# Attention in a Perceiver block: softmax weights stationary, values streaming

## The chip, the cores and the metric

The kernel runs on one core of a Trainium2 chip. The metric is device microseconds of one execution; three runs of the kernel before took 2517.41, 2518.72 and 2515.10, median 2517.41. Each TensorE product here is a stationary operand (loaded into the array by its own instruction, LDWEIGHTS) and a moving operand that streams past, column by column, into PSUM.

## The reference, cut to what matters

The block is a cross attention from 512 latent tokens to 8192 context tokens, then a state-space (Mamba) layer, a gated MLP and a mixture of experts. Only the attention changes:

```python
# Q: normalised latents (1, 512, 512); K = V = context (1, 8192, 512); 16 heads of 64
q = (scale * (Q @ Wq + bq)).reshape(bs, q_len, NH, DM)
k = (K @ Wk + bk).reshape(bs, kv_len, NH, DM)
v = (V @ Wv + bv).reshape(bs, kv_len, NH, DM)
a = jax.nn.softmax(jnp.einsum('nlhd,nshd->nhls', q, k), axis=-1)
o = jnp.einsum('nhls,nshd->nlhd', a, v).reshape(bs, q_len, NH * DM)
return o @ Wo + bo
```

Everything is kept near float32 accuracy on a float16 array: each operand is split into a high half and a low half (the rest), both float16, and a product is high x high, high x low and low x high (`three`, `product`).

## The kernel before, in words

Scratch memory in DRAM passes results between stages. `latent_queries` makes the queries, `context_keys_values` makes keys and values of all 8192 context tokens in 16 chunks of 512 (`kd` and `vd`, high and low halves, and a row maximum per query for the softmax), `attention` follows, then the Mamba stage, the MLP and the experts. Each engine runs its own program, written by hand in order; semaphores hold it where it needs another's result.

In `attention` a head has 32 steps (`HP`), each of two key tiles of 128 keys against all 512 queries. For a step:

- TensorE makes the scores of both tiles (`scores`, L938 and L939), keys stationary, queries moving: four matmuls of 512 columns into one of three PSUM buffers `st`.
- ScalarE takes the exponential of the two tiles in one operation of 1024 columns into `pf` (float32, a ring of 4 steps, `FULL`), L771.
- The high half `ph` (a ring of 8, `RING`) is a copy to float16: ScalarE in even steps (L765), VectorE in odd ones (L814, `DVE_HI`). The low half `pl` is `pf - ph`, always VectorE, L818.
- TensorE adds weights times values (`values`): values stationary, weights moving. The stationary block of a key tile is 128 columns, 64 of the value's high half and 64 of its low half: two 512-column matmuls with `ph` (L900); four with `pl` and 32 columns of the high half each, in four column strips of the array (L907); and four with a block of ones, which give the softmax's sums (L915).

TensorE works by groups of four steps (`SP`): the scores of a group, then the values of the group before (`LAG` = 1 group). A loop over the heads runs from one cut in a head to the same cut in the next (`turns`, `pair_turns`), so a head's end lies inside the next head's steps.

At a head's end VectorE copies the accumulator to SBUF (L824, L825). SP's queue sends the sums to DRAM and the two halves of the output to `a0` and `a1`; once per pair of heads the sums come back spread over partitions, VectorE adds them and takes the reciprocal, SP spreads it over 64 partitions each, and VectorE and ScalarE scale the output and split it into `oh` and `ol` (`reciprocals`, `scale`, `high`, `low`). After the last head `oh` and `ol` are projected with 96 matmuls on TensorE, and normalisation follows.

SP's queue loads the next head's keys and values in quarters, as the present head is done with them (L635, L640). In the first head the same queue also holds the other heads' queries, the biases and a zero fill of `xs_dram` for the experts (L653 to L659).

Of the kernel before, what the change touches and what calls it, by code (L numbers as in the profile page):

```python
# [90 lines left out]
WT = TW * (NCK // 2 - 1)  # L91

# [166 lines left out]
def context_keys_values(nc, keep, ctxT, q_dram, kd, vd, m_dram, mrow, m_out, wpack, wsplit):  # L259
# [6 lines left out]
    with ExitStack() as ctx:  # L266
# [4 lines left out]
        vs = [m.sb(f"vs{i}", [P, NH, CK // P, 2 * DH], F16) for i in range(2)]  # L271
# [11 lines left out]
        made = m.sem("made")  # L283
# [33 lines left out]
        def _(sp):  # L317
# [12 lines left out]
            def chunk(g, par, i, tiles, more):  # L330
# [6 lines left out]
                at = g * CK if isinstance(g, int) else i * (2 * CK) + (2 - par) * CK  # L337

                for js in (range(0, 6), range(6, 8)) if isinstance(g, int) and g == NCK - 1 else (range(0, 8),):
# [4 lines left out]
                    sp.dma_start(vd.rearrange("h p s -> p h s")[:, :, bass.ds(at + kts.start * P, len(js) // 2 * P)],  # L344
# [9 lines left out]
            for e in range(TW):  # L354
                load_weights(0, e)
            chunk(0, 0, None, (), True)
# [14 lines left out]
        def _(pool):  # L371
            def chunk(g, par, uses, i, tiles):
                nxt = 1 - par
                for n in range(8):
# [11 lines left out]
                    nc.gpsimd.tensor_tensor(vs[par][:, hs, kt, DH:2 * DH],  # L386
# [8 lines left out]

            identity(nc, pool, ident, made)
# [154 lines left out]
FULL = 4  # L551

SUMS_AT, SCALE_AT, HIGH_AT, LOW_AT, CUT = 8, 14, 16, 18, 20
EPS1, EPS2 = 1e-5, 1e-6
LAG = 1

HP = KT // 2
SP = 4
HS = HP // SP

# [3 lines left out]
DVE_HI = (1, 3, 5, 7)  # L564


def act_highs(n):

    return n // 8 * (8 - len(DVE_HI)) + sum(k not in DVE_HI for k in range(n % 8))


def attention(nc, keep, x, q_dram, m_dram, mrow, m_out, kd, vd, sums, r_dram, bv, bo, n1w, wsplit, xs_dram):
# [3 lines left out]
    with ExitStack() as ctx:  # L576
# [4 lines left out]
        vs = m.sb("vs", [P, KT, P], F16)  # L581
        ones = m.sb("ones", [P, 32], F16)
        pf = m.sb("pf", [P, FULL, 2, T])
        ph, pl = (m.sb(n, [P, RING, 2, T], F16) for n in ("ph", "pl"))
        parts = m.sb("parts", [P, 2, T])
# [4 lines left out]
        both = [m.sb(n, [P, 2, TT]) for n in ("both_var", "both_sd", "both_rs", "both_tmp")]  # L590
        oh, ol = (keep.big[0][:, i * 2 * WC:(i + 1) * 2 * WC].rearrange("p (j t) -> p j t", t=T) for i in range(2))
        a0, a1, rb, bob = (keep.big[1][:, i * 2 * T:(i + 1) * 2 * T].bitcast(F32) for i in range(4))
        dn = keep.big[1][:, 8 * T:8 * T + 64].bitcast(F32).rearrange("p (n c) -> p n c", c=8)
# [13 lines left out]
        pl_ready, pv_done, acc_read, o_out = (m.sem(n) for n in ("pl_ready", "pv_done", "acc_read", "o_out"))  # L607
        dn_in, r_ready, r_out, rb_in = m.sem("dn_in"), m.sem("r_ready"), m.sem("r_out"), m.sem("rb_in")
        own_dve, consts, vec_in, small_in = m.sem("own_dve"), m.sem("consts"), m.sem("vec_in"), m.sem("small_in")
        s_ready, oh_ready, ol_ready, y_ready = m.sem("s_ready"), m.sem("oh_ready"), m.sem("ol_ready"), m.sem("y_ready")  # L610
# [11 lines left out]
        FK = SP * 2 * P  # L622
# [8 lines left out]
        def _(sp):  # L631
# [7 lines left out]
            def load_values(n, q):  # L639
                sp.dma_start(vs[:, q * 2 * QP:(q + 1) * 2 * QP, :].rearrange("p k c -> p (k c)"),  # L640
                             vd.rearrange("h p s -> p h s")[:, bass.ds(n, 1), q * QK:(q + 1) * QK]
                             .rearrange("p h s -> p (h s)")).then_inc(v_in[q], 16)
# [19 lines left out]
            def load_next(h):  # L662
# [6 lines left out]
            def store(j, e):  # L669

                h = 2 * j + e
                sp.wait_ge(acc_read, 2 * h + 4)
                sp.dma_start(sums[:, bass.ds(h * T, T)],
                             parts[0:P:32, 1, :]).then_inc(o_out, 16)
                for n, a in enumerate((a0, a1)):
                    sp.dma_start(a[e * DH:(e + 1) * DH, :], parts[n * DH:(n + 1) * DH, 0, :]).then_inc(o_out, 16)

            def factors(j):


                sp.wait_ge(o_out, j * 96 + 144)
                sp.dma_start(dn, sums.rearrange("n (j p c) -> j p n c", p=P, c=8)[bass.ds(j, 1)]
                             .rearrange("o p n c -> p (o n) c")).then_inc(dn_in, 16)
                sp.wait_ge(r_ready, j + 1)
                sp.dma_start(r_dram.rearrange("(j p c) -> j p c", p=P, c=8)[bass.ds(j, 1)]
                             .rearrange("o p c -> p (o c)"), dn[:, 0, :]).then_inc(r_out, 16)
                sp.wait_ge(r_out, j * 16 + 16)
                for e in range(2):
                    sp.dma_start(rb[e * DH:(e + 1) * DH, :],
                                 r_dram[bass.ds(j * (2 * T) + e * T, T)].partition_broadcast(DH)).then_inc(rb_in, 16)  # L690

            with sp.Fori(0, PAIRS - 1) as j:
                for e in range(2):
                    load_next(2 * j + e)
                    store(j, e)
                factors(j)
            load_next(NH - 2)
            store(PAIRS - 1, 0)
            sp.wait_ge(st_ready, (NH - 1) * HP + 2 * QP)
            load_split(sp, wsplit, W.O, k_cur[:, 0:2 * WC], k_one[:, 0:2 * WC], w_in)  # L700
            sp.wait_ge(pl_ready, NH * HP + RING)
            sp.dma_start(xs, x.rearrange("(t p) d -> p t d", p=P)).then_inc(small_in, 16)
            store(PAIRS - 1, 1)
            factors(PAIRS - 1)
# [6 lines left out]
        def _(pool):  # L711
            own = Chain(pool, const_ready)
            own.done(nc.gpsimd.memset(ones[:, :], 1.0))
# [7 lines left out]
        def turns(eng, step, steps, cut, end=None):  # L721


            for s in range(cut):
                step(0, s)
            with eng.Fori(0, NH - 1) as h:
                for s in range(cut, steps + cut):
                    step(h, s)
                if end:
                    end(h)  # L730
            for s in range(cut, steps):
                step(NH - 1, s)
            if end:
                end(NH - 1)

        def pair_turns(eng, step, end, late, once):

            for s in range(CUT):  # L740
                step(0, s)
            once()
            with eng.Fori(0, PAIRS - 1) as j:
                for e in range(2):
                    for s in range(CUT, HP + CUT):
                        step(2 * j + e, s)
                        if s == HP + 2:
                            end(2 * j + e)
                        if e and s - HP in late:
                            late[s - HP](j)  # L750
            for s in range(CUT, HP + CUT):
                step(NH - 2, s)
                if s == HP + 2:
                    end(NH - 2)
            for s in range(CUT, HP):
                step(NH - 1, s)
            end(NH - 1)

        @block.scalar
        def _(act):  # L760
            def hi(h, s):
                g = h * HP + s
                act.wait_ge(pf_ready, g + 1)
                act.wait_ge(pv_done, g + 1)
                nc.scalar.activation(ph[:, s % RING, :, :], pf[:, s % FULL, :, :], ACT.Copy).then_inc(ph_ready, 1)  # L765
# [10 lines left out]
            def high(j):  # L776
                act.wait_ge(s_ready, j + 1)
                nc.scalar.activation(oh[:, bass.ds(j, 1), :].rearrange("p o t -> p (o t)"), a0, ACT.Identity,
                                     bias=bvs[:, bass.ds(j, 1)]).then_inc(oh_ready, 1)
# [5 lines left out]
            pair_turns(act, pair, lambda h: None, {HIGH_AT: high}, lambda: act.wait_ge(consts, 2))  # L785
            high(PAIRS - 1)
# [7 lines left out]
        def _(dve):  # L794
# [14 lines left out]
            def pair(h, s):  # L809
                g = h * HP + s  # L810
                if s % 8 in DVE_HI:
                    dve.wait_ge(pf_ready, g + 1)
                    dve.wait_ge(pv_done, g + 1)
                    nc.vector.tensor_copy(ph[:, s % RING, :, :], pf[:, s % FULL, :, :]).then_inc(ph_own, 1)  # L814
                    dve.wait_ge(ph_own, h * (HP - act_highs(HP)) + s + 1 - act_highs(s + 1))
                else:
                    dve.wait_ge(ph_ready, h * act_highs(HP) + act_highs(s + 1))
                nc.vector.tensor_tensor(pl[:, s % RING, :, :], pf[:, s % FULL, :, :], ph[:, s % RING, :, :],  # L818
                                        ALU.subtract).then_inc(pl_ready, 1)
# [1558 lines left out]
```

## Time and profile before

| | us |
|---|---|
| median of three runs (lowest, highest) | 2517.41 (2515.10, 2518.72) |
| span of the profiled execution | 2515.4 |
| TensorE busy in the span | 2395.6 (95%) |
| VectorE busy | 1974.4 (78%) |
| ScalarE busy | 1603.1 (64%) |

The profiled execution has no time of its own beside its span, which lies among the three runs. A matmul's record of 0.38 us at 512 columns includes its way through the array; from start to start it is 0.216. "Idle before" is an engine's idle time ahead of a group, with what ended it. In a timeline "x16" after a row merges that many instructions into one row, and PEld is the loading of weights.

### The profile page before, as it was taken

How to read it: one execution, taken by the hardware profiler on the slowest of the kernel's cores; microseconds unless marked ns; L12 is line 12 of the kernel's file. 1: busy time of each engine (PE TensorE's matmuls, PEld its weight loads, DVE VectorE, ACT ScalarE, POOL GpSimd, SP SyncE). 2: the span in 40 equal slices, each digit the busy share in tenths (PEclk: the TensorE clock that was granted, in tenths of full speed). 3: DMA queues.
4: the chain of work that ended last, by engine and by line, in shares of the span. 5: the costliest groups of instructions: out<-in, count | busy, mean ns of one | idle time of the engine just before them, and what ended most of it. 6: DMA issues, size and time to landing. Idle time of an engine off the chain costs nothing. (4 is left out here: it accounts for less than half of the span.)

```text
span 2515.4 us, 39361 instructions
## 1 busy us (share of the span) xinstructions
PE 2395.6 (95%) x14111; PEld 1015.0 (40%) x14111; DVE 1974.4 (78%) x1972; ACT 1603.1 (64%) x1974; POOL 672.5 (27%) x461
## 2 busy tenths in 40 slices
PE   7999999999999799999999999999887878999999
PEld 3333333333333244444444444444332333444554
DVE  5777777777777788888888898888679994267996
ACT  5555555565555478777788777888375442137994
POOL 1455555555555400000000000000019990010001
PEclk9999999999999899999999999999999899999999
DMA  7245654455445593433433333333231005139994
GB/s 251 84 151 163 204 167 150 153 173 175 150 133 150 139 267 89 113 102 95 108 88 105 96 100 92 104 94 107 93 138 52 0 0 201 56 146 346 405 405 174
DMA packets 178205, 366.02 MB, mean 146 GB/s; under 512 B 19545, under 2 KB 90329, under 8 KB 174425
## 3 DMA queue, kind: packets, MB, share of 16 engines
q1 hardware_dynamic: 176610, 360.81, 45.1%
q0 software_dynamic: 1280, 4.20, 0.5%
q8 instruction: 38, 0.62, 0.1%
q14 instruction: 29, 0.24, 0.0%
q10 hardware_dynamic: 248, 0.15, 0.0%
HBM read 254.24 MB, written 106.68 MB: 143 GB/s over the span
## 5 line engine op out<-in xcount | busy, mean ns | idle before, releaser
L466 DVE TENSOR_REDUCE kv_mx<-kv_s 128x1024 f32 (+1 forms) x512 | 595.6, 1218 | 222.5 <-PE kv_s L502 222.5
L818 DVE TENSOR_TENSOR at_pl<-at_pf,at_ph 128x1024 f16<-128x1024 f32 x512 | 613.2, 1223 | 113.2 <-ACT at_ph L765 104.4
L771 ACT ACTIVATE at_pf<-at_st 128x1024 f32<-128x1024 f32 x512 | 497.3, 1025 | 187.2 <-PE at_st L939 182.2
L938 PE MATMUL at_st<-keep_big,at_k_cur 128*128 (+1 forms) x1024 | 390.5, 381 | 10.0 <-DMA keep_big<-q_dram 7.1
L939 PE MATMUL at_st<-keep_big,at_k_one 128*128 (+1 forms) x1024 | 388.9, 380 | 0.0
L765 ACT ACTIVATE at_ph<-at_pf 128x1024 f16<-128x1024 f32 x256 | 272.9, 1066 | 0.0
L1135 POOL MEMSET mamba_zero<- 128x2 f32 x1 | 0.1, 100 | 939.8 <-POOLq L60 939.8
L900 PE MATMUL at_acc<-at_ph,at_vs 128*128 128x512 f16 x1024 | 242.4, 379 | 2.9 <-DVE at_pl L818 2.8
L382 POOL TENSOR_TENSOR kv_ksl<-kv_kf,kv_ksh 128x512 f16<-128x512 f32 x128 | 148.0, 1156 | 246.4 <-ACT kv_ksh L410 246.4
L1049 PE MATMUL kv_kp<-first_ch,first_wkh 128*128 128x512 f16 x512 | 195.0, 381 | 4.2 <-DVEq L448 4.2
L407 ACT ACTIVATE kv_kf<-kv_kp,first_bks 128x512 f32<-128x512 f32 x128 | 87.4, 683 | 169.7 <-PE kv_kp L1049 169.7
L1049 PE MATMUL kv_kp<-first_ch,first_wkl 128*128 128x512 f16 x512 | 195.1, 381 | 0.0
L1049 PE MATMUL kv_vp<-first_wvh,first_ch 128*128 128x512 f16 x512 | 194.5, 380 | 0.3 <-DVE kv_mx L466 0.3
L1049 PE MATMUL kv_kp<-first_cl,first_wkh 128*128 128x512 f16 x512 | 194.8, 380 | 0.0
L1049 PE MATMUL kv_vp<-first_wvl,first_ch 128*128 128x512 f16 x512 | 194.6, 380 | 0.0
L1049 PE MATMUL kv_vp<-first_wvh,first_cl 128*128 128x512 f16 x512 | 194.2, 379 | 0.0
L414 ACT ACTIVATE kv_vf<-kv_vp 128x512 f32<-128x512 f32 x128 | 76.1, 594 | 184.6 <-PE kv_vp L1049 184.6
L386 POOL TENSOR_TENSOR kv_vs<-kv_vf,kv_vs 128x512 f16<-128x512 f32 x128 | 148.0, 1156 | 129.7 <-ACT kv_vs L416 129.7
L1516 PE MATMUL ms_yp<-ms_hc,keep_ident 128*128 128x512 f32 x256 | 133.6, 664 | 46.1 <-POOL ms_hc L1380 33.7
L814 DVE CAST at_ph<-at_pf 128x1024 f16<-128x1024 f32 x256 | 177.3, 693 | 0.0
L938 PEld LDWEIGHTS at_st<-keep_big,at_k_cur 128*128 128x128 f16 x1024 | 100.2, 98 | 171.7 <-issue 54.6
L1392 POOL TENSOR_TENSOR ms_b<-mamba_u,keep_big 128x1024 f32<-128x1024 f32 x63 | 146.5, 2353 | 55.8 <-DVE ms_b L1448 55.3
(351 smaller groups left out, 3859.7 us busy)
## 6 DMA issues: line engine op xcount, KB each, us to landing
keep_big<-gate_up SPq DMA_DIRECT2D x17, 2048.0 KB, 13.1
at_vs<-vd SPq DMA_DIRECT2D x64, 512.0 KB, 3.9
at_k_cur<-kd SPq DMA_DIRECT2D x126, 256.0 KB, 3.8
vd<-kv_vs SPq DMA_DIRECT2D x15, 2048.0 KB, 7.7
kv_tf<-wpack SPq DMA_DIRECT2D x21, 1024.0 KB, 6.4
keep_big<-down SPq DMA_DIRECT2D x17, 1024.0 KB, 13.2
first_cf<-ctxT SPq DMA_DIRECT2D x16, 1024.0 KB, 12.9
ex_yg<-gate_up SPq DMA_DIRECT2D x8, 2048.0 KB, 13.4
```

Of the source, the lines that this page charges most:

```text
L382: nc.gpsimd.tensor_tensor(ksl[par][:, n, :], kf[:, n % 4, :], ksh[par][:, n, :], ALU.subtract).then_inc(kl_ready, 1)
L386: nc.gpsimd.tensor_tensor(vs[par][:, hs, kt, DH:2 * DH], vf[:, n % 4, :].rearrange("p (h d) -> p h d", d=DH), vs[par][:, hs, kt, 0:DH], AL ...
L466: nc.vector.reduce_max(mx[:, bass.ds(g * (NH * TT) + 2 * (m - TT), 2)], s1[:, m % 3, :, :], AX.X).then_inc(s1_max, 1)
L765: nc.scalar.activation(ph[:, s % RING, :, :], pf[:, s % FULL, :, :], ACT.Copy).then_inc(ph_ready, 1)
L771: nc.scalar.activation(pf[:, s % FULL, :, :], st[:, s % HP % NST, :, :], ACT.Exp, scale=SCORE).then_inc(pf_ready, 1)
L814: nc.vector.tensor_copy(ph[:, s % RING, :, :], pf[:, s % FULL, :, :]).then_inc(ph_own, 1)
L818: nc.vector.tensor_tensor(pl[:, s % RING, :, :], pf[:, s % FULL, :, :], ph[:, s % RING, :, :], ALU.subtract).then_inc(pl_ready, 1)
L900: nc.tensor.matmul(acc[:, 0, :], vs[:, 2 * s + e, :], ph[:, s % RING, e, :], start=(s == 0 and e == 0), stop=False)
L938: nc.tensor.matmul(st[:, w % NST, e, :], k_cur[:, tile], qh[:, q], start=True, stop=False)
L939: last = nc.tensor.matmul(st[:, w % NST, e, :], k_one[:, tile], ql[:, q], start=False, stop=True)
L1049: last = nc.tensor.matmul(out, a, b, start=(start and n == 0), stop=(stop and n == len(pairs) - 1))
L1392: nc.gpsimd.tensor_tensor(b[i % RB][:, :, :], u[:, :].unsqueeze(1).to_broadcast([P, HN, T]), bb[q], ALU.mult).then_inc(b_ready, 1)
```

## The change

Weights of the softmax become stationary and values move. For each key tile and each of four blocks of 128 queries (`own_acc[t]`, two to a PSUM bank) the high half is loaded and 130 columns stream past it: 64 of the value's high half, a one, a zero, and 64 of the low half. Then the low half is loaded and the first 65 of these columns stream. The column of ones gives the sums, so the four matmuls with ones go, and the output has queries on partitions. The key stage stores values in rows of 130 (`VW`) and fills ones and zeros once. TensorE goes step by step, six steps (`LAG`) between a step's scores and its values. The halves are made for two steps at once, in operations of 2048 columns: ScalarE copies even pairs, VectorE odd ones; `pf` has 8 steps.

```diff
+VW = 2 * DH + 2
+ONE = DH
...
-                    nc.gpsimd.tensor_tensor(vs[par][:, hs, kt, DH:2 * DH],
+                    nc.gpsimd.tensor_tensor(vs[par][:, hs, kt, ONE + 2:VW],
...
+            sp.wait_ge(unit_ready, 4)
+            for v in vs:
+                nc.gpsimd.memset(v[:, :, :, ONE:ONE + 1], 1.0).then_inc(unit_ready, 1)
+                nc.gpsimd.memset(v[:, :, :, ONE + 1:ONE + 2], 0.0).then_inc(unit_ready, 1)
...
-FULL = 4
+FULL = 8
-LAG = 1
+LAG = 6
...
+        own_acc = [acc[:, t // 2, t % 2 * VW:(t % 2 + 1) * VW] for t in range(TT)]
+        oT = [st[:, 2, 0, :], st[:, 2, 1, :]]
...
             def pair(h, s):                                        # ScalarE
                 g = h * HP + s
                 act.wait_ge(st_ready, g + 1)
-                act.wait_ge(pl_ready, g + 1 + RING - FULL)
+                if s % 2 == 0:
+                    act.wait_ge(pl_ready, h * (HP // 2) + s // 2 + 1)
                 nc.scalar.activation(pf[:, s % FULL, :, :], st[:, s % HP % NST, :, :], ACT.Exp, ...)
-                if s and (s - 1) % 8 not in DVE_HI:
-                    hi(h, s - 1)
+                if s >= 2 and s % 4 == 2:
+                    hi(h, s // 2 - 1)
...
             def pair(h, s):                                        # VectorE
+                if s % 2 == 0:
+                    return
+                p, at = s // 2, (s - 1) % RING
+                if p % 2:
+                    dve.wait_ge(pf_ready, h * HP + s + 1)
+                    dve.wait_ge(pv_done, h * HP + s + 1)
+                    nc.vector.tensor_copy(ph[:, at:at + 2, :, :], pf[:, at:at + 2, :, :]).then_inc(ph_own, 1)
+                    dve.wait_ge(ph_own, h * (HP // 4) + p // 2 + 1)
+                else:
+                    dve.wait_ge(ph_ready, h * (HP // 4) + p // 2 + 1)
+                nc.vector.tensor_tensor(pl[:, at:at + 2, :, :], pf[:, at:at + 2, :, :], ph[:, at:at + 2, :, :],
                                         ALU.subtract).then_inc(pl_ready, 1)
             def end(h):                           # after the pair of steps 32, 33
                 dve.wait_ge(pv_done, h * HP + HP + RING)
-                dve.wait_ge(o_out, h * 48 + 48)
-                nc.vector.tensor_copy(parts[:, 0, :], acc[:, 0, :]).then_inc(acc_read, 1)
-                nc.vector.tensor_copy(parts[:, 1, :], acc[:, 1, :]).then_inc(acc_read, 1)
+                for b in range(2):
+                    nc.vector.tensor_copy(av[:, 2 * b:2 * b + 2, :], acc[:, b, 0:2 * VW]...).then_inc(acc_read, 1)
+                dve.wait_ge(acc_read, h * 2 + 4)
+                nc.vector.tensor_tensor(osum[:, :, :], av[:, :, 0:DH], av[:, :, ONE + 2:VW], ALU.add)...
+                nc.vector.reciprocal(rc[:, :], av[:, :, ONE]).then_inc(sum_ready, 1)
+                dve.wait_ge(sum_ready, h * 2 + 2)
+                nc.vector.tensor_tensor(o[:, :, bass.ds(h * DH, DH)], osum[:, :, :],
+                                        rc[:, :].unsqueeze(2).to_broadcast([P, TT, DH]), ALU.mult)...
...
+            def values(h, s):                                      # TensorE
+                if s % QP == 0:
+                    pe.wait_ge(v_in[s // QP], 16 * (h + 1))
+                pe.wait_ge(pl_ready, h * (HP // 2) + s // 2 + 1 + RING // 2)
+                for e in range(2):
+                    for t in range(TT):
+                        tok = slice(t * P, (t + 1) * P)
+                        first = s == 0 and e == 0 and t % 2 == 0
+                        if first:
+                            pe.wait_ge(acc_read, h * 2 + 1 + t // 2)
+                        nc.tensor.matmul(own_acc[t], ph[:, s % RING, e, tok], vs[:, 2 * s + e, :], start=first, ...)
+                        last = nc.tensor.matmul(own_acc[t][:, 0:ONE + 1], pl[:, s % RING, e, tok],
+                                                vs[:, 2 * s + e, 0:ONE + 1], start=False, ...)
+                last.then_inc(pv_done, 1)
```

The trip of the sums through DRAM, `sums`, `r_dram`, `parts` and the work per pair of heads go. Instead `end` leaves the scaled output `o` of every head in SBUF, queries on partitions, and it is transposed after the last head, on TensorE (`turn`: four float32 transposes per pair of heads, into the third score buffer), split by ScalarE and VectorE, and projected:

```diff
+            turn(0)
+            turn(1)
+            for s in range(HP - LAG, HP):
+                values(NH - 1, s)
...
+            for j in range(LATE):
+                project(j, range(TT))
+                turn(j + 2)
+            for t in range(TT):
+                for j in range(LATE, PAIRS):
+                    project(j, (t,))
```

VectorE's order there is `low(0)`, `low(1)`, the last head's `end`, `low(2)` to `low(6)`, four additions of the bias to the block's input, `low(7)`. In the head loop VectorE's `end(h)` stands at step 33 (`END_AT` = 1), and ScalarE's wait for the scaled biases moves behind the loop.

## Rows read from the trace of the kernel before

**Rows 1.** Windows: busy us of each engine, granted clock (PEclk), DMA share, GB/s.
```profile
868.30:1789.00 920.70, 914.79 (x7168) 386.85 (x7168) 804.39 (x849) 728.49 (x775) 13.83 (x9) 1.00 0.41 110
...
2239.80:2241.10 1.30, 1.26 (x48) 1.30 (x49) 0.00 (x0) 1.29 (x1) 1.29 (x35) 0.50 0.35 38
```

**Rows 2.** Timeline of TensorE, one group: start us, us, engine, line, operation, count.
```profile
1398.78 0.39 PE L938 MATMUL at_st<-keep_big,at_k_cur 128*128 x1
...
1402.25 1.89 PE L900 MATMUL at_acc<-at_ph,at_vs 128*128 128x512 f16 x8
1404.07 1.05 PE L907 MATMUL at_acc<-at_pl,at_vs 128*32 128x512 f16 x16
...
1405.91 0.39 PE L938 MATMUL at_st<-keep_big,at_k_cur 128*128 x1
```

**Rows 3.** Timeline of the router's matmuls and their weight loads.
```profile
2239.84 1.43 PE L1049 MATMUL ex_up<-keep_router,keep_hidden 128*128 128x16 f16 x48 [1.72 <-PEq L60]
...
2239.80 1.37 PEld L1049 LDWEIGHTS ex_up<-keep_router,keep_hidden 128*128 128x128 f16 x48 [2.09 <-issue]
```

**Rows 4.** Chain of waits, experts: start us, us, engine, tile, line, count.
```profile
2287.25 0.44 PE ex_up L2220 x4
2287.69 2.59 PE ex_up L1049 x12
...
2290.28 0.45 PE ex_gp L2200 x8
```

**Rows 5.** Groups by form: operands, count | busy us, mean ns | idle before.
```profile
L771 ACT ACTIVATE at_pf<-at_st 128x1024 f32<-128x1024 f32 x512 | 497.3, 1025 | 187.2 <-PE at_st L939 182.2 <-DVE at_nws L806 3.8 <-DVE at_pl L818 1.2
L434 ACT ACTIVATE kv_th<-kv_tf 128x2048 f16<-128x2048 f32 x21 | 39.8, 1893 | 0.0
L765 ACT ACTIVATE at_ph<-at_pf 128x1024 f16<-128x1024 f32 x256 | 272.9, 1066 | 0.0
...
L818 DVE TENSOR_TENSOR at_pl<-at_pf,at_ph 128x1024 f16<-128x1024 f32 x512 | 613.2, 1223 | 113.2 <-ACT at_ph L765 104.4
L814 DVE CAST at_ph<-at_pf 128x1024 f16<-128x1024 f32 x256 | 177.3, 693 | 0.0
L198 DVE SCALAR_TENSOR_TENSOR lq_wl<-lq_wf,lq_wh 128x2048 f16<-128x2048 f32 x2 | 4.6, 2288 | 1.5 <-ACT lq_wh L167 1.5
L824 DVE COPY at_parts<-at_acc 128x512 f32<-128x512 f32 x16 | 10.9, 684 | 2.6 <-PE at_acc L915 2.6
...
L1049 PE MATMUL ex_up<-keep_router,keep_hidden 128*128 128x16 f16 x48 | 1.4, 174 | 1.7 <-PEq L60 1.7
```

**Rows 6.** Timeline of ScalarE and VectorE in that group of steps.
```profile
1399.93 1.94 ACT L771 ACTIVATE at_pf<-at_st 128x1024 f32<-128x1024 f32 x2 [1.47 <-PE at_st L939]
...
1402.85 1.23 DVE L818 TENSOR_TENSOR at_pl<-at_pf,at_ph 128x1024 f16<-128x1024 f32 x1 [0.97 <-ACT at_ph L765]
1403.99 0.69 DVE L814 CAST at_ph<-at_pf 128x1024 f16<-128x1024 f32 x1
1404.71 2.36 DVE L818 TENSOR_TENSOR at_pl<-at_pf,at_ph 128x1024 f16<-128x1024 f32 x2
```

**Rows 7.** Timeline at the attention's start and at head 1.
```profile
868.40 0.61 PE L938 MATMUL at_st<-keep_big,at_k_cur 128*128 128x512 f16 x1 [7.07 <-DMA keep_big<-q_dram]
...
871.62 0.38 PE L938 MATMUL at_st<-keep_big,at_k_cur 128*128 128x512 f16 x1
...
913.42 0.54 SPq L635 DMA_DIRECT2D at_k_one<-kd  x1
...
928.42 0.39 PE L938 MATMUL at_st<-keep_big,at_k_cur 128*128 x1
```

**Rows 8.** Landing of that key load, tile at_k_one, 912 to 914 us.
```profile
DMA to landing us min/median/max: 11.7/11.7/11.7
```

**Rows 9.** Timeline of TensorE, first and last matmul of the 96 projecting.
```profile
1789.01 0.39 PE L1049 MATMUL at_st<-at_k_cur,keep_big 128*128 128x512 f16 x1
...
1809.61 0.38 PE L1049 MATMUL at_st<-at_k_cur,keep_big 128*128 128x512 f16 x1
```

More of the change, by code:

```diff
@@ L270, in context_keys_values @@
         ksh, ksl = ([m.sb(f"{n}{i}", [P, PAIRS, CK], F16) for i in range(2)] for n in ("ksh", "ksl"))
[L271 removed]
+        vs = [m.sb(f"vs{i}", [P, NH, CK // P, VW], F16) for i in range(2)]
         tf = [m.sb(f"tf{i}", [P, WC]) for i in range(TW)]
@@ L549, with attention @@
 RING = 8
-FULL = 4
-SUMS_AT, SCALE_AT, HIGH_AT, LOW_AT, CUT = 8, 14, 16, 18, 20
+FULL = 8
 EPS1, EPS2 = 1e-5, 1e-6
-LAG = 1
+LAG = 6
 HP = KT // 2
-SP = 4
-HS = HP // SP
 NST = 3
 NQ = 4
[L564 to L572, printed above, removed]
+def attention(nc, keep, x, q_dram, m_dram, mrow, m_out, kd, vd, bv, bo, n1w, wsplit, xs_dram):
     with ExitStack() as ctx:
@@ L667, in load_next @@
                     load_values(h + 1, q)
[L669 to L698, printed above, removed]
             sp.wait_ge(st_ready, (NH - 1) * HP + 2 * QP)
             load_split(sp, wsplit, W.O, k_cur[:, 0:2 * WC], k_one[:, 0:2 * WC], w_in)
-            sp.wait_ge(pl_ready, NH * HP + RING)
+            sp.wait_ge(pl_ready, NH * (HP // 2) + RING // 2)
             sp.dma_start(xs, x.rearrange("(t p) d -> p t d", p=P)).then_inc(small_in, 16)
-            store(PAIRS - 1, 1)
-            factors(PAIRS - 1)
             sp.wait_ge(st_ready, NH * HP)
@@ L719, in _, with turns, hi @@
             identity(nc, pool, ident, made)
-        def turns(eng, step, steps, cut, end=None):
+        def turns(eng, step, cut, end=None, once=None):
             for s in range(cut):
                 step(0, s)
+            if once:
+                once()
             with eng.Fori(0, NH - 1) as h:
-                for s in range(cut, steps + cut):
+                for s in range(cut, HP + cut):
                     step(h, s)
-                if end:
-                    end(h)
-            for s in range(cut, steps):
+                    if end and s == HP + END_AT:
+                        end(h)
+            for s in range(cut, HP):
                 step(NH - 1, s)
[L733 to L757, printed above, removed]
+        END_AT, CUT = 1, 20
         @block.scalar
         def _(act):
[L761 to L765, printed above, removed]
+            def hi(h, p):
+                at = 2 * p % RING
+                act.wait_ge(pf_ready, h * HP + 2 * p + 2)
+                act.wait_ge(pv_done, h * HP + 2 * p + 2)
+                nc.scalar.activation(ph[:, at:at + 2, :, :], pf[:, at:at + 2, :, :], ACT.Copy).then_inc(ph_ready, 1)
             def pair(h, s):
@@ L784, in _ @@
             act.dma_start(ql[DH:DH + 1, 0:T], mrow[0:TT, :]).then_inc(q_in, 16)
-            pair_turns(act, pair, lambda h: None, {HIGH_AT: high}, lambda: act.wait_ge(consts, 2))
-            high(PAIRS - 1)
+            turns(act, pair, CUT)
+            act.wait_ge(consts, 2)
+            for j in range(PAIRS):
+                act.wait_ge(oT_ready, j + 1)
+                nc.scalar.activation(oh[:, j, :], oT[j % 2], ACT.Identity, bias=bvs[:, j:j + 1]).then_inc(oh_ready, 1)
             act.wait_ge(var_ready, 1)
@@ L846, in low @@
                                                ALU.add, ALU.subtract).then_inc(ol_ready, 1)
-            pair_turns(dve, pair, end, {SUMS_AT: reciprocals, SCALE_AT: scale, LOW_AT: low}, scaled)
-            reciprocals(PAIRS - 1)
+            turns(dve, pair, CUT, end, scaled)
+            low(0)
+            low(1)
+            end(NH - 1)
+            for j in range(2, PAIRS - 1):
+                low(j)
             dve.wait_ge(small_in, 32)
@@ L942, in step, with turn, project @@
             def step(h, d):
-                ahead, w = divmod(d, HS)
-                for s in range(SP * w, SP * (w + 1)):
-                    scores(h, ahead, s)
+                ahead, w = divmod(d, HP)
+                scores(h, ahead, w)
                 if d >= LAG:
                     values(h, d - LAG)
-            pe.wait_ge(q_in, 64)
-            turns(pe, step, HS, LAG)
-            for d in range(HS - LAG, HS):
-                values(NH - 1, d)
+            def turn(j):
+                pe.wait_ge(o_ready, 2 * j + 2)
+                if j >= 2:
+                    pe.wait_ge(ol_ready, j - 1)
+                for t in range(TT):
+                    last = nc.tensor.transpose(oT[j % 2][:, t * P:(t + 1) * P], o[:, t, j * P:(j + 1) * P], ident[:, :])
+                last.then_inc(oT_ready, 1)
+            def project(j, ts):
+                pe.wait_ge(ol_ready, j + 1)
+                for t in ts:
+                    tok = slice(t * P, (t + 1) * P)
+                    last = product(nc, yp[t], three(oh[:, j, tok], ol[:, j, tok], woh[:, j, :], wol[:, j, :]),
+                                   start=(j == 0), stop=(j == PAIRS - 1))
+                    if j == PAIRS - 1:
+                        last.then_inc(y_ready, 1)
+            pe.wait_ge(q_in, 64)
+            turns(pe, step, LAG)
+            pe.wait_ge(made, 2)
+            pe.wait_ge(pf_ready, NH * HP - 2)
+            turn(0)
+            turn(1)
+            for s in range(HP - LAG, HP):
+                values(NH - 1, s)
             pe.wait_ge(pf_ready, NH * HP)
@@ L2313, in program @@
         keep.router = [m.sb(f"router{i}", [P, DC, NE], F16) for i in range(2)]
-        attention(nc, keep, x, q_dram, m_dram, mrow, m_out, kd, vd, sums, r_dram, bv, bo, n1w, wsplit, xs_dram)
+        attention(nc, keep, x, q_dram, m_dram, mrow, m_out, kd, vd, bv, bo, n1w, wsplit, xs_dram)
         with ExitStack() as inner:
```

112 lines of the change are left out of this document (29 added, 83 removed).

## The prediction

> **What bounds the kernel now.** I read the busy time by stretches first. In the attention's stretch, from 868.3 to 1789.0 us, TensorE is busy for 914.8 of 920.7 us at full granted clock, VectorE for 804 and ScalarE for 728 [rows 1]. So TensorE sets the pace here, and the reader is to see that the other two have a reserve of 13% and 21%. Then I read TensorE's order of time. A group of four steps starts at 1398.78 and the next at 1405.91, so it takes 7.13 us: scores 3.47, the high halves' values 1.82, the rest (low halves and sums, four column strips side by side) 1.84 [rows 2]. That is 1.782 us a step and 8 x 7.13 = 57.04 a head. No matmul of these waits: exponentials and halves come early. What follows the attention is untouched, so every microsecond of its end moves the whole.
>
> **Values: the term that decides.** A step has two key tiles. Before, values and sums cost 1.82 + 1.84 = 3.66 us in four steps, 0.915 a step. After, each key tile has four token tiles, each with a load of 128x128 weights and 130 columns (high) and another load and 65 columns (low): 16 loads, 8 x 195 = 1560 columns a step. The trace has no row of 65 or 130 columns. Twelve 512-column matmuls take 2.59 us, 0.2157 each; eight of 128 columns, each with its own 128x128 load, take 0.45, 0.056 each [rows 4]. A straight line through both gives 0.416 ns a column and 2.5 ns for a matmul: 0.0567 us for 130, 0.0296 for 65. It holds only if a load hides beside 65 columns. For this the nearest row is the router's: 48 matmuls of 16 columns with 48 loads lie in 1.43 us; without the last one's own 0.174, (1.43 - 0.174) / 47 = 26.7 ns for load and matmul together [rows 3, 5], and the granted clock was 0.50 there, the lower of its two levels, 1.2 GHz [rows 1], so a load at 2.4 GHz is hardly longer. 29.6 is above 26.7, hence I take full cover: 8 x (0.0567 + 0.0296) = 0.690 a step. The end above: every matmul at the 128-column row, 8 x (0.0567 + 0.056) = 0.901; further above, loads not covered at all, 16 x 0.0267 on top of 0.690 = 1.117. The end below is the columns alone, 1560 x 0.416 ns = 0.649. Those 16-column products also accumulate into one place back to back, so a low matmul behind its high one on the same columns should not wait.
> The Trainium skill, "TensorE: Matmul & The Clock Gate", section "Back-to-back issue gap", speaks against this: it gives some 81 ns a matmul for a sustained stream of load and 128-column matmul, and calls 56 ns the isolated gap. By it each of the 16 pairs would be longer by about 25 ns, an estimate of 0.40 us a step; the bursts of eight here are at 56, but no row shows a long one.
> Scores are unchanged, 3.47 / 4 = 0.8675. The step becomes 0.8675 + 0.690 = 1.557 us, a head 32 x 1.557 = 49.8.
>
> **The halves.** ScalarE: an exponential follows another at 1.94 - 1.025 = 0.915 us [rows 5, 6]; a 2048-column copy lasts 1.89 (the weights' split, L434). Four steps: 4 x 0.915 + 1.89 = 5.55, against 6.23 of TensorE. VectorE: 1223 ns for 1024 and 2288 ns for 2048 columns [rows 5], so a wide subtraction takes 2.29 and holds the engine 2.20 (a narrow one 1403.99 - 1402.85 = 1.14, 0.08 less than it lasts [rows 6]). The 1024-column cast lasts 0.693; with the subtraction's fixed 0.16 (2 x 1223 - 2288), 2048 columns last 0.16 + 2 x 0.533 = 1.23, at most 2 x 0.693 = 1.39; a dependent operation starts 0.03 later [rows 6]. Four steps: 2.20 + 1.26 + 2.20 = 5.66. Both stay below TensorE.
>
> **Lag six.** From the start of a group of four steps (t = 0): an exponential starts 1399.93 - 1398.78 = 1.15 us after the first of its step's four score matmuls [rows 2, 6], so the third step's at 2 x 1.557 + 1.15 = 4.26; the wide copy lies at 5.18 to 7.07; the first pair's subtraction at 7.10 to 9.39; the cast, behind it on VectorE, at 9.30 to 10.53; the second subtraction at 10.56 to 12.85. TensorE wants the first pair at 6 x 1.557 + 0.87 = 10.21 and the second at 8 x 1.557 + 0.87 = 13.32. With 0.05 for the signal the slack is 0.77 and 0.42 us: no wait, but a thin margin. With every wide operation at twice the narrow row (2.13 copy, 1.39 cast, 2.45 subtraction, [rows 5]) the second pair is ready at 13.6 and the step becomes (13.6 - 0.87) / 8 = 1.59.
>
> **End of a head.** VectorE now runs five operations behind the pair of steps 32 and 33: it waits for the last value (about 38 x 1.557 + 0.2, 0.2 us after it would be free), two copies of 260 columns (0.42 each by the 512-column 0.684, holding 0.34), an addition of 256 columns (0.42), a reciprocal of four columns (0.20, hardly more than the fixed 0.16) and a product (0.42) [rows 5]. Queued behind them is the next cast: it starts some 1.93 us late, so the pair of steps 34 and 35 is late by 1.93 - 0.42 = 1.5 us, and TensorE waits that long once in a head. The copies themselves end in time, since scores lie before the next head's first value. 15 heads x 1.5 = 22 us; from 0, if the margin is larger than computed, to 2.8, if the scores' 0.87 cover none of it.
> What goes: the trip of sums through memory and the scaling per pair of heads. VectorE's and SP's work there lay beside TensorE, so its removal is worth nothing.
>
> **First head.** TensorE would reach head 1 at about 868.4 + 50 = 918. Its first keys' last part was issued at 913.42, behind the zero fill of `xs_dram` in SP's queue, and landed after 11.7: 925.1 [rows 7, 8]. Before, head 1 began at 928.42 and hid that. It now waits some 7 us, and that idle time has a price: after the 7.07 us idle before 868.40 the first matmul's record is 0.61 instead of 0.38 and eight of them take 3.22 instead of 1.73 [rows 7], 1.5 us lost. Head 1 then runs from 925.3 + 1.5 = 926.8.
>
> **Drain and tail.** After the last score: two turns (0.88, four float32 transposes in 0.44 [rows 4]), then six steps' values, of which the last pair waits for its halves at 28 x 1.557 + 12.9, 6.7 us after the last step; with two steps' values 8.0 in all. The projection of 96 matmuls took 1809.61 + 0.22 - 1789.01 = 20.8 us [rows 9]; six turns are now between its parts, 6 x 0.44 = 2.6, and the last head's low half stands behind four additions on VectorE, about 1.3 more: 3.9 longer.
>
> **Elsewhere.** Rows of 1040 instead of 1024 bytes to memory and 4160 instead of 4096 back: 1.6% more bytes beside a busy TensorE. The four memsets run while GpSimd waits for its first key. Both nothing; if the last store of the key stage were exposed, under 1 us.
>
> **Sum.** Before, the last value ended at 1789.0, where the projection starts [rows 9]. After: 926.8 + 15 x (49.8 + 1.5) + 8.0 = 1704.3. Gained 84.7, given back 3.9: 80.8 us from a span of 2515.4, 2434.6. The runs' median is 2517.4, 2.0 above that span; I predict 2437 us.
>
> **Rivals.** (1) The weight load has a floor of 56 ns, so that 65 columns cost as much as 128. For it: no row between 16 and 128 columns. Against it: the 26.7 ns. Step 0.8675 + 0.901 = 1.769, head 56.6; the end's wait is swallowed by the margin. 15 x 0.44 + 3 at head 1 less 3.9: about 2512.
> (2) The other side: loads of weights stand in the stream of matmuls, since all stationary operands are now fresh and the streams are short. Place: values on TensorE; price: up to 26.7 ns x 16 = 0.427 a step; it decides from (1.782 - 1.557) / 16 = 14 ns a matmul. At the full price the step is 1.984, a head 63.5, 16 x 6.4 + 3.9: about 2624. Against it: the 0.45 us for eight pairs with loads. The Trainium skill's sustained figure, from the section named above, would come near this, as an estimate of 2610.
> (3) The halves are late each step, the wide operations being as dear as two narrow ones, or signals longer than 0.05: step 1.59 to 1.63 and 1.9 at each end, 16 to 36 us more by heads of 32 steps and 6 at the ends: 2459 to 2479. For it: a margin of 0.42 us. Against: the 2048-column rows.
> (4) No wait at the heads' ends: 2415.
>
> **Chances.** Forecast 0.64 (own range 2418 to 2455), (1) 0.07, (2) 0.10, (3) 0.14, (4) 0.05. The range 2408 to 2492 holds the forecast, (3) and (4), 0.83 less their edges. About 0.2% (5 us) is what a measurement can tell from none. Faster by more: 0.64 + 0.14 + 0.05 + half of (1) = 0.86; same 0.04; slower 0.10.
>
> **What will show it.** On TensorE: starts of successive value matmuls 57 and 30 ns apart, a step of 1.56, every head alike at about 51.3 us, with one wait for at_pl near the sixth step. VectorE: cast 1.23, subtraction 2.29; ScalarE: copy 1.89. A wait for keys of about 7 us near 918 with half the granted clock behind it. A wait for at_pl in every group says (3); 85 ns or more for each pair's low part says (2). I am wrong if a step isn't 1.52 to 1.62 us.

## The result, and the profile after

The changed kernel takes 2442.09 us (median of four runs, 2440.62 to 2443.37); the kernel before 2516.95 (median of four runs on the same chip). The ratio is 0.970, with a 95% interval of 0.969 to 0.972. The profiled execution's span is 2438.9 us, against 2515.4. I had predicted 2437 (2408 to 2492).

Of the page of the changed kernel, the span and the costliest groups of the attention (columns as in [rows 5], without forms):

```profile
span 2438.9 us, 44693 instructions
...
L762 DVE TENSOR_TENSOR at_pl<-at_pf,at_ph 128x2048 f16<-128x2048 f32 x256 | 585.5, 2292 | 77.1 <-ACT at_ph L708 72.8
...
L837 PE MATMUL at_acc<-at_vs,at_ph 128*128 128x130 f16 x4096 | 425.1, 220 | 25.0 <-DVE at_pl L762 24.9
...
L839 PE MATMUL at_acc<-at_vs,at_pl 128*128 128x65 f16 x4096 | 411.4, 192 | 0.0
...
L708 ACT ACTIVATE at_ph<-at_pf 128x2048 f16<-128x2048 f32 x128 | 243.5, 1902 | 0.0
```

A matmul's record (220, 192 ns) overlaps the next ones, which start some 57 and 30 ns later; what it costs is the distance between starts. Those stand in TensorE's timeline at the end of a head, to be read beside [rows 2]:

```profile
1300.30 0.38 PE L864 MATMUL at_st<-keep_big,at_k_one 128*128 x1
1302.14 0.23 PE L837 MATMUL at_acc<-at_vs,at_ph 128*128 128x130 f16 x1 [1.46 <-DVE at_pl L762]
...
1303.71 0.22 PE L837 MATMUL at_acc<-at_vs,at_ph 128*128 128x130 f16 x1
1303.77 0.19 PE L839 MATMUL at_acc<-at_vs,at_pl 128*128 128x65 f16 x1
1303.80 0.22 PE L837 MATMUL at_acc<-at_vs,at_ph 128*128 128x130 f16 x1
...
1304.41 0.38 PE L863 MATMUL at_st<-keep_big,at_k_cur 128*128 x1
...
1305.97 0.38 PE L863 MATMUL at_st<-keep_big,at_k_cur 128*128 x1
```

Sixteen value matmuls take 1304.41 - 1303.71 = 0.70 us, a step 1305.97 - 1304.41 = 1.56. Once in a head TensorE stands still: 1.84 us between starts instead of 0.22, so 1.62 lost. It waits for the lower halves (`at_pl`), and VectorE's timeline of that stretch says why:

```profile
1294.29 2.29 DVE L762 TENSOR_TENSOR at_pl<-at_pf,at_ph 128x2048 f16<-128x2048 f32 x1 [0.74 <-ACT at_ph L708]
1296.73 0.77 DVE L768 COPY at_av<-at_acc 128x260 f32<-128x260 f32 x2
1297.53 0.43 DVE L771 TENSOR_TENSOR at_osum<-at_av 128x256 f32<-128x256 f32 x1
1297.88 0.17 DVE L772 RECIPROCAL at_rc<-at_av 128x4 f32<-128x4 f32 x1
1298.20 0.43 DVE L774 TENSOR_TENSOR keep_big<-at_osum,at_rc 128x256 f32 x1
1298.54 1.22 DVE L758 CAST at_ph<-at_pf 128x2048 f16<-128x2048 f32 x1
1299.79 4.49 DVE L762 TENSOR_TENSOR at_pl<-at_pf,at_ph 128x2048 f16<-128x2048 f32 x2
```

The five closing operations fill 1296.73 to 1298.54; only then come the cast and the subtraction that TensorE wants. A second, smaller loss stands in the waits of the attention (waited for: us in total, times, longest): the scores of each head's second step wait for an exponential. (The weight loads that wait for the copies out of the accumulators, the second line, cost nothing: the matmul behind them starts on time, 0.22 us after the one before it.)

```profile
PEld at_st L863 <- ACT at_pf L715: 3.6, 15, 0.3
PEld at_acc L837 <- DVE at_av L768: 2.1, 14, 0.2
```
```profile
1285.86 1.90 ACT L708 ACTIVATE at_ph<-at_pf 128x2048 f16<-128x2048 f32 x1
1287.65 1.93 ACT L715 ACTIVATE at_pf<-at_st 128x1024 f32<-128x1024 f32 x2
...
1288.72 0.10 PEld L863 LDWEIGHTS at_st<-keep_big,at_k_cur 128*128 128x128 f16 x1 [0.24 <-ACT at_pf L715]
```

Three score buffers don't divide a head's 32 steps. At the turn of a head the kernel therefore uses a buffer again after two steps instead of three, so the second step needs the exponential of step 31, and that one stands behind ScalarE's wide copy.

Head 1's keys, to be read beside [rows 7]: SP's issue, TensorE's first score, and the windows behind it (granted clock 0.50, then 0.96).

```profile
893.94 0.67 SPq L657 DMA_DIRECT2D xs_dram<-at_none  x1
894.98 15.76 SPq L633 DMA_DIRECT2D at_k_cur<-kd  x2
910.85 0.54 SPq L633 DMA_DIRECT2D at_k_one<-kd  x1
```
```profile
923.00 0.60 PE L863 MATMUL at_st<-keep_big,at_k_cur 128*128 x1 [3.03 <-DMA at_k_one<-kd]
```
```profile
923.00:926.00 3.00, 3.00 (x20) 1.95 (x21) 2.97 (x2) 1.00 (x1) 0.00 (x0) 0.50 1.04 217
926.00:929.00 3.00, 3.00 (x38) 1.98 (x36) 0.45 (x1) 1.24 (x3) 0.00 (x0) 0.96 1.03 218
```

And the drain, up to the first matmul that projects, which was at 1789.01 [rows 9]:

```profile
1704.48 0.23 PE L837 MATMUL at_acc<-at_vs,at_ph 128*128 128x130 f16 x1 [0.68 <-DVE at_pl L762]
1707.94 0.23 PE L837 MATMUL at_acc<-at_vs,at_ph 128*128 128x130 f16 x1 [1.90 <-DVE at_pl L762]
...
1709.35 0.38 PE L992 MATMUL at_st<-at_k_cur,keep_big 128*128 128x512 f16 x1
```

The attention ends 79.7 us earlier; what follows it takes 3.2 longer (2438.9 - 1709.35 against 2515.4 - 1789.01), which leaves 76.5 of the span.

### The profile page after: what moved, and what is told of

It is laid out like the page before. It is cut to its first block and busy times, and to the rows that moved or that the text cites. A ratio compares the mean times of both kernels' runs of the same rounds, so it can differ in the third digit from the quotient of the medians.

```text
span 2438.9 us, 44693 instructions
## 1 busy us (share of the span) xinstructions
PE 2295.8 (94%) x17215; PEld 1190.2 (49%) x17215; DVE 1930.3 (79%) x1588; ACT 1600.6 (66%) x1846; POOL 669.1 (27%) x464
## 5 line engine op out<-in xcount | busy, mean ns | idle before, releaser
L762 DVE TENSOR_TENSOR at_pl<-at_pf,at_ph 128x2048 f16<-128x2048 f32 x256 | 585.5, 2292 | 77.1 <-ACT at_ph L708 72.8
L715 ACT ACTIVATE at_pf<-at_st 128x1024 f32<-128x1024 f32 x512 | 504.7, 1022 | 112.9 <-PE at_st L864 112.7
L837 PE MATMUL at_acc<-at_vs,at_ph 128*128 128x130 f16 x4096 | 425.1, 220 | 25.0 <-DVE at_pl L762 24.9
L837 PEld LDWEIGHTS at_acc<-at_vs,at_ph 128*128 128x128 f16 x4096 | 367.5, 97 | 92.0 <-DVE at_pl L762 32.8
L839 PE MATMUL at_acc<-at_vs,at_pl 128*128 128x65 f16 x4096 | 411.4, 192 | 0.0
L839 PEld LDWEIGHTS at_acc<-at_vs,at_pl 128*128 128x128 f16 x4096 | 362.0, 98 | 57.3 <-issue 0.3
L708 ACT ACTIVATE at_ph<-at_pf 128x2048 f16<-128x2048 f32 x128 | 243.5, 1902 | 0.0
```

Source lines behind the costliest of these rows:

```text
L708: nc.scalar.activation(ph[:, at:at + 2, :, :], pf[:, at:at + 2, :, :], ACT.Copy).then_inc(ph_ready, 1)
L762: nc.vector.tensor_tensor(pl[:, at:at + 2, :, :], pf[:, at:at + 2, :, :], ph[:, at:at + 2, :, :], ALU.subtract).then_inc(pl_ready, 1)
L837: nc.tensor.matmul(own_acc[t], ph[:, s % RING, e, tok], vs[:, 2 * s + e, :], start=first, stop=False, skip_group_check=True)
L839: last = nc.tensor.matmul(own_acc[t][:, 0:ONE + 1], pl[:, s % RING, e, tok], vs[:, 2 * s + e, 0:ONE + 1], start=False, stop=(s == HP - 1 a ...
```

## Experiments

My theory: the gain is the columns that TensorE no longer streams, all loads hidden; the wide (2048-column) halves only keep pace, thanks to lag six; what is lost are VectorE's closing operations and the late keys. Its rivals: a weight load sets a floor, or the wide halves carry the gain. Every kernel is the changed one with the edit shown (cut with "..."), unless it says otherwise; all ratios are to the kernel before.

**More columns** (e1_low130):
```diff
-nc.tensor.matmul(own_acc[t][:, 0:ONE + 1], pl[...], vs[:, 2 * s + e, 0:ONE + 1], ...)
+nc.tensor.matmul(own_acc[t], pl[...], vs[:, 2 * s + e, :], ...)
```


> The low half's matmul streams all 130 columns instead of 65, so it adds the product of low weight and low value to the result. Theory (the gain is the columns that TensorE no longer streams, with every weight load hidden): 8 x 65 more columns a step at 0.416 ns are 0.216 us, the step becomes 1.56 + 0.22 = 1.78 us; with so slow a step the margin of lag six grows, so the 1.6 us wait at a head's end disappears; 512 x 0.216 - 16 x 1.8 = 82, so about 2515 to 2528 us. Rival (a load of 128x128 weights sets the floor of a short matmul, 65 columns cost what 128 do): the step stays at 1.56 and the time at 2442 us.

2535.37 us, ratio 1.006 (1.005 to 1.008). The step is 1.77. TensorE's timeline, two steps' first scores:
```profile
1300.00 0.38 PE L863 MATMUL at_st<-keep_big,at_k_cur 128*128 x1
...
1301.77 0.38 PE L863 MATMUL at_st<-keep_big,at_k_cur 128*128 x1
...
1348.13 0.23 PE L837 MATMUL at_acc<-at_vs,at_ph 128*128 128x130 f16 x1 [1.04 <-DVE at_pl L762]
```
Sixty-five more columns on half of the matmuls use up the whole gain: between 65 and 130 columns there is no floor, the columns are what is paid. The time lies 7 us above my range, because the wait at a head's end shrank only to 1.04 and didn't go: VectorE's closing operations wait for the last value, which a slower TensorE brings later too.

**Less ahead of the cast** (e2_split_end):
```diff
+            def sums(h):
 ...
+            def scale(h):
 ...
-turns(dve, pair, CUT, end, scaled)
+turns(dve, pair, CUT, {1: end, 3: sums, 5: scale}, scaled)
```


> Behind the pair of steps 32 and 33 VectorE does only the two copies out of the accumulators; the addition and the reciprocal follow the pair of steps 34 and 35, the product the pair of 36 and 37. Theory (TensorE waits at a head's end because five VectorE operations stand ahead of the next cast): 1.0 us less ahead of that cast, the wait falls from 1.6 to about 0.6 us, 15 x 1.0 = 15 us less, 2424 to 2432 us; a little of it may come back as a wait at the next pair. Rival (the wait comes from the accumulators, which have to be read before the next head's values can start, or from the two copies alone): 2442 us.

2430.66 us, ratio 0.965 (0.963 to 0.966). The wait is now this, once a head (0.72 us between starts instead of 0.22, and 0.15 more two pairs on):
```profile
1297.35 0.23 PE L843 MATMUL at_acc<-at_vs,at_ph 128*128 128x130 f16 x1 [0.34 <-DVE at_pl L762]
...
1348.18 0.23 PE L843 MATMUL at_acc<-at_vs,at_ph 128*128 128x130 f16 x1 [0.34 <-DVE at_pl L762]
```
A head takes 50.83 us instead of 51.80, so 15 us are won in 15 heads, as expected. The median fell by 11. In the profiled execution head 1's keys came 2.7 us later (a wait of 5.75), and what follows the attention took 2.9 us longer. Of these, 1.2 are the projection's, at whose start the granted clock was 0.60 (the window below, columns as in [rows 1]) where the changed kernel had 1.00; the rest is open.
```profile
1697.00:1700.00 3.00, 3.00 (x32) 1.98 (x29) 2.18 (x7) 0.00 (x0) 0.00 (x0) 0.60 0.74 189
```
The closing operations are the wait's cause.

**Keys ahead of the zero fill** (e3_fill_later), SP's queue:
```diff
-sp.wait_ge(none_ready, 1)
-sp.dma_start(xs_dram.rearrange("(s p) n -> p s n", p=P), none[:, :]...)
 ...
+sp.wait_ge(none_ready, 1)
+sp.dma_start(xs_dram.rearrange("(s p) n -> p s n", p=P), none[:, :]...)
 sp.wait_ge(st_ready, (NH - 1) * HP + 2 * QP)
```

> The zero fill of xs_dram is issued behind the head loop instead of ahead of head 1's keys. Theory (head 1's keys land late because their issue stands behind the fill in SP's queue): the keys land before TensorE has finished head 0, the 3.0 us wait for them and the half granted clock behind it (some 1.4 us) go, about 2437.5 us. Rival (the issue is held by head 0's queries or by SP's own pace): the wait stays, 2442 us.

2437.15 us, ratio 0.968 (0.966 to 0.969). SP issues the first `at_k_one` at 895.75 instead of 910.85, and no wait for keys is left. The two issues ahead of it took 15.76 us behind the fill and take 1.38 without it.
```profile
894.28 1.38 SPq L633 DMA_DIRECT2D at_k_cur<-kd  x2
895.75 0.54 SPq L633 DMA_DIRECT2D at_k_one<-kd  x1
```
Of the 5 us, 3.0 are the wait and some 1.3 the half clock behind it.

**Lag five** (e4_lag5):
```diff
-LAG = 6
+LAG = 5
```

> The lag between a step's scores and its values is five steps instead of six, all else as in the changed kernel. Theory (the wide operations keep pace only by lag six, with 0.4 to 0.8 us to spare): the values want each pair 1.56 us earlier, so TensorE waits in each group of four steps for the second pair, about 0.6 to 1.1 us a group, or the step becomes what the chain allows: 2500 to 2560 us. Rival (the reserve lies elsewhere, lag six is more than needed): 2442 us within 5.

2531.22 us, ratio 1.005 (1.004 to 1.007): one step less lag gives back the whole gain. TensorE, then VectorE:
```profile
1304.98 0.23 PE L837 MATMUL at_acc<-at_vs,at_ph 128*128 128x130 f16 x1 [0.30 <-DVE at_pl L762]
1308.44 0.23 PE L837 MATMUL at_acc<-at_vs,at_ph 128*128 128x130 f16 x1 [0.17 <-DVE at_pl L762]
```
```profile
1302.63 2.29 DVE L762 TENSOR_TENSOR at_pl<-at_pf,at_ph 128x2048 f16<-128x2048 f32 x1 [1.30 <-ACT at_ph L708]
```
Nearly every pair waits (206 of 256), and four steps take 7.05 us instead of 6.23 (3.46 and 3.59 for two). VectorE itself is idle for 1.30 us in four steps, waiting for ScalarE's wide copy: what is late is the chain, not an engine that is full.

**Narrow halves** (e5_narrow): ScalarE and VectorE go back to the operations of the kernel before, 1024 columns for one step (two key tiles, where the expectation says a key tile); the streaming values, lag six and the end of a head stay.
```diff
-nc.scalar.activation(ph[:, at:at + 2, :, :], pf[:, at:at + 2, :, :], ACT.Copy)
+nc.scalar.activation(ph[:, s % RING, :, :], pf[:, s % FULL, :, :], ACT.Copy)
...
-nc.vector.tensor_tensor(pl[:, at:at + 2, :, :], pf[:, at:at + 2, :, :], ph[:, at:at + 2, :, :], ALU.subtract)
+nc.vector.tensor_tensor(pl[:, s % RING, :, :], pf[:, s % FULL, :, :], ph[:, s % RING, :, :], ALU.subtract)
```


> The changed kernel with its halves made as before, by 1024-column operations a key tile (ScalarE's and VectorE's casts in the old alternation), lag six and the streaming values kept. Theory (the gain is TensorE's; the wide halves only keep pace): the step stays at 1.56, VectorE has some 6.0 us of work per four steps against 6.23, and the end of a head costs about as much as now; 2434 to 2455 us. Rival (the wide operations carry the gain): VectorE cannot keep pace, the step becomes 1.6 or more, over 2465 us.

2414.79 us, ratio 0.959 (0.958 to 0.961): 27 us faster than the changed kernel, and below all that I expected. Busy time from 960 to 1680 us (TensorE, loads, VectorE, ScalarE), of the changed kernel and of this one:
```profile
960.00:1680.00 720.00, 698.26 (x8899) 482.59 (x8896) 658.75 (x405) 626.74 (x557) 0.00 (x0) 1.00 0.37 101
```
```profile
960.00:1680.00 720.00, 719.30 (x9256) 502.15 (x9255) 709.14 (x765) 663.24 (x692) 0.00 (x0) 1.00 0.38 103
```
VectorE is busier, 709 of 720 us, and yet TensorE doesn't stop: 719.3 for 698.3. Between 1300 and 1352 us no start on TensorE is late. The wait for halves at a head's end is gone although the five closing operations still stand in VectorE's queue, and so is the one for exponentials, since no 1.90 us copy delays them. So the wide halves do not merely keep pace; they cost 27 us, although this kernel waited 7.28 us for head 1's keys and the changed one 3.03. They save VectorE some 4% of its work (47.4 us a head for 49.1), which nobody waited for, and make each half wait for two steps' exponentials.

**Wide halves alone** (e6_before_wide): the kernel before with the changed kernel's `hi` and `pair` (its lag is one group of four steps, where the expectation says eight groups).
```diff
-FULL = 4
+FULL = 8
 ...
-nc.vector.tensor_tensor(pl[:, s % RING, :, :], pf[:, s % FULL, :, :], ph[:, s % RING, :, :], ALU.subtract)
+nc.vector.tensor_tensor(pl[:, at:at + 2, :, :], pf[:, at:at + 2, :, :], ph[:, at:at + 2, :, :], ALU.subtract)
```

> The kernel before with one part of the change alone: halves made for two key tiles by 2048-column operations; its values (weights streaming, four strips) and its lag of eight groups stay. Theory: TensorE sets the pace at 1.782 us a step and the halves lay beside it, so nothing is gained, 2510 to 2530 us. Rival (the wide halves carry the gain): near 2442 to 2480 us.

2565.74 us, ratio 1.019 (1.017 to 1.021): I expected no change, and it is 48 us slower. TensorE at the end of a head, and VectorE ahead of its wait:
```profile
1303.67 1.03 PE L903 MATMUL at_acc<-at_ph,at_vs 128*128 128x512 f16 x4
1305.93 1.04 PE L903 MATMUL at_acc<-at_ph,at_vs 128*128 128x512 f16 x4 [1.23 <-DVE at_pl L821]
```
```profile
1301.13 0.69 DVE L827 COPY at_parts<-at_acc 128x512 f32<-128x512 f32 x1
1301.73 0.68 DVE L828 COPY at_parts<-at_acc 128x512 f32<-128x512 f32 x1
1302.33 1.22 DVE L817 CAST at_ph<-at_pf 128x2048 f16<-128x2048 f32 x1
1303.58 2.29 DVE L821 TENSOR_TENSOR at_pl<-at_pf,at_ph 128x2048 f16<-128x2048 f32 x1
```
The wide cast and subtraction stand behind the two copies out of the accumulator, and TensorE waits for them. The group of four steps takes 8.53 us there; two groups in every second head, where VectorE's products for a pair of heads stand ahead of the cast, take 7.73 and 8.00; the others take 7.13 or 7.33. In the kernel before, the group with the two copies takes 7.13 like any other. So a lag of one group nearly carries the wide operations alone, and has no room for anything else in VectorE's queue.

**Sixteen columns** (e7_low16):
```diff
-nc.tensor.matmul(own_acc[t][:, 0:ONE + 1], pl[...], vs[:, 2 * s + e, 0:ONE + 1], ...)
+nc.tensor.matmul(own_acc[t][:, 0:16], pl[...], vs[:, 2 * s + e, 0:16], ...)
```

> The low half's matmul streams 16 columns instead of 65, so most of the low correction is left out of the result; all loads stay. It shows what a load of 128x128 weights costs at the full clock when almost nothing covers it. If load and short matmul take 26.7 ns together, as the router's rows at the lower clock, the pair is 0.0567 + 0.0267, the values 0.667 a step, the step 1.535, and about 2428 to 2435 us. If a load at the full clock takes half of that, TensorE's own pace would be 1.43 a step and VectorE's 5.7 us per four steps would still let it come near; the time is then set by the halves, 2390 to 2430 us, and the starts of successive value matmuls in the trace are 57 and 13 ns apart. If the load has a floor of 56 ns nothing is different from 2442 us.

2429.25 us, ratio 0.965 (0.963 to 0.967). A step, and the sixteen value matmuls in it:
```profile
1310.37 0.22 PE L837 MATMUL at_acc<-at_vs,at_ph 128*128 128x130 f16 x1
...
1311.03 0.38 PE L863 MATMUL at_st<-keep_big,at_k_cur 128*128 x1
...
1311.89 0.22 PE L837 MATMUL at_acc<-at_vs,at_ph 128*128 128x130 f16 x1
```
The pair takes (1311.03 - 1310.37) / 8 = 82.5 ns, so load and 16 columns together take 26 beside the 56.7 of 130 columns: the first of the three cases, with a step of 1.52. That is the router's 26.7 at half the granted clock [rows 3]: this floor did not fall when the clock doubled. Whether the load or the short matmul sets it is not shown. The 65 columns, with 30, lie just above it.

**The wide version mended** (e8_all): the edits of e2 and e3, and in the tail
```diff
-project(j, range(TT))
 turn(j + 2)
+project(j, range(TT))
```

> The changed kernel with the split end of a head, the zero fill behind the head loop, and in the tail the turn of pair j+2 ahead of the projection of pair j. Theory (the three waits are separate and their gains add): -11 from the split, -5 from the fill, 0 to -1 from the turns: about 2425 us, 2421 to 2430. Rival (one wait takes the other's place, since both let head 1 start earlier against the same VectorE): 2430 us or more.

2422.91 us, ratio 0.963 (0.961 to 0.964): the gains add: 19 us, where e2 and e3 had 11 and 5. No run has the edit of the turns alone; what it brings can be read in the next experiment.

**The narrow version mended** (e9_narrow_fill): e5 with e3's edit and e8's in the tail, both as shown above.

> Halves made step by step (1024 columns) as in the run before, and with it the zero fill behind the head loop and the turn of pair j+2 ahead of the projection of pair j. Theory (with narrow halves TensorE waits for nothing in the head loop but head 1's keys, 7.3 us there, with half a granted clock behind it): -7.3 -1.4 -1, about 2405 us, 2402 to 2409. Rival (VectorE, which is nearly full with narrow halves, is the bound, and the time won at the keys comes back as waits for halves): 2411 us or more.

2405.78 us, ratio 0.955 (0.954 to 0.957), the fastest of all. Two scores 32 steps apart:
```profile
1301.11 0.38 PE L868 MATMUL at_st<-keep_big,at_k_cur 128*128 x1
...
1351.01 0.38 PE L868 MATMUL at_st<-keep_big,at_k_cur 128*128 x1
```
A head takes 49.90 us, 1.559 a step, as the line through the columns gave (1.557), and at a head's end TensorE waits for nothing. The projection's matmuls start within 22.7 us, in e5 within 24.2: 1.5 come from the turns.

**Narrow halves with less lag** (e10_narrow_lag5, e11_narrow_lag4): e5 with
```diff
-LAG = 6
+LAG = 5    # e11: 4
```

> Narrow halves (1024 columns a step) with lag five. With 2048-column operations lag five cost 89 us. Theory (it is the length of the wide operations' chain, which waits for two steps' exponentials, that uses up the lag): a narrow chain is ready some 4.5 us after its step's first score, lag five wants it at 8.7, so nothing waits in a step: 2411 to 2420 us. Rival (any halves need lag six, since VectorE is behind by its load): 2440 us or more.

2414.60 us, ratio 0.959 (0.957 to 0.960): the same as with lag six. With wide halves the same step cost 89 us. So it is the length of the wide chain that needs lag six.

> Narrow halves with lag four, where values want a step's halves 7.1 us after its first score. Theory: still behind the 4.5 us of the chain, and the last value of a head, for which VectorE waits, comes a step earlier too, so that the end of a head costs no more: 2410 to 2425 us. Rival (lag is needed in full): 2460 us or more.

2430.92 us, ratio 0.966 (0.964 to 0.968): 16 us slower, 6 beyond my range. The wait that appears isn't for halves:
```profile
1343.97 0.23 PE L842 MATMUL at_acc<-at_vs,at_ph 128*128 128x130 f16 x1 [0.84 <-DVE at_av L773]
```
The next head's first value waits for VectorE's copies out of the accumulators, 1.00 us between starts beyond the usual 0.22, 15 times.

## Why the prediction was right, and where it was not

The sum predicted 80.8 us of the span; 76.5 came. By its steps:

**Values.** Right: 0.70 for 0.690, a step of 1.56 for 1.557. The straight line through 128 and 512 columns held at 130 and 65, and e1 and e7 show both of its ends: columns are paid, and a load with only 16 columns to cover it takes 26 ns with its matmul, not 56 (rival 1), nor do loads come on top of the stream (rival 2). The Trainium skill, "TensorE: Matmul & The Clock Gate", section "Back-to-back issue gap", gives some 81 ns for each load with 128 columns in a sustained stream; here 8192 matmuls with their loads, in runs of sixteen between scores that load weights too, kept some 57 (130 columns) and 30 ns (65) through 840 us, and the trace decides.

**Halves and lag.** The durations were right (cast 1.22 for 1.23, subtraction 2.29, copy 1.90 for 1.89), and so was the thin margin: no wait inside a head, and e4, which takes 1.56 of it away, waits in nearly every pair. What I did not price is what the wide halves themselves cost against narrow ones under the same streaming values. I took the pieces of the change as one, and called them needed in the theory; e5, e6 and e10 show that they are not.

**End of a head.** The place, cause (e2) and count were right, the size too small: 1.62 against 1.5, since the cast began 2.0 late for the 1.93 counted, with the margin of 0.42 as computed. Beside it stand 0.24 for the scores of each head's second step, which wait for an exponential behind the wide copy. I had looked at ScalarE's wide copy only for the halves behind it, and not at the score buffers. With the step's rounding a head took 51.80 for 51.3, 7.5 us in 15 heads.

**First head.** Right in kind, wrong in size: the wait was 3.0, not 7, because the keys were issued at 910.85 instead of 913.42 and because TensorE came to head 1 at 920.0 instead of 918 (its attention began at 869.23, and head 0 took 50.7). In other executions the wait was 5.75 (e2), 7.28 (e5), 6.6 (e10) and 6.0 (e11), with the keys issued between 912.3 and 914.3: it depends on when SP's queue gets past the fill and when TensorE arrives. Head 1 ran from some 924.3 instead of 926.8 (its third step began at 927.68, and in an undisturbed head the third step begins 3.39 after the first). These 2.5 us to the good are this execution's luck. The half clock behind the idle stretch was there.

**Drain and tail.** 8.0 for 8.0 (1709.35 less 924.3 and 15 x 51.80); the tail 3.2 for 3.9.

So -7.5, +2.5 and +0.7 make the 4.3 us by which the span missed; the total is closer than its terms. The parts of the change, by e5 and the medians: streaming values with lag six and the new end of a head gave some 102 us (2517 to 2415), which no run takes apart further, and the wide halves took 27 of them back. That split was not in the prediction; the total was.

## What to carry to other kernels

When short streams with a fresh weight load each replace long ones, price the columns by a line through two forms that the trace has, and check it against the nearest row for a load with nothing to hide it. A wider operation saves its engine a fixed part, but makes the consumer wait for all of its inputs: before widening, ask whether the engine was the bound, and count the margin in steps at the worst place, which is the end of a loop, where other work stands in the same queue. Undo each part of a change that gained: here one part was hidden behind another's gain.

## What the runs showed of the hardware

A matmul of 16 columns with its own 128x128 load took 26 ns at the full granted clock in e7 (1.00, 2.4 GHz) and 26.7 at the half one [rows 3]: twice the clock brought no more there. And VectorE busy for 709 of 720 us (e5) held nobody up inside the loop, while at 659 (the changed kernel) TensorE waited 28 us, 15 x (1.62 + 0.24): a busy share says little where the order in a queue decides.
